# A graph convolution on one core: the shared row is handed on by four products on 32-column tiles instead of one of 128 columns

## What is computed

```python
h = jax.nn.silu(edge_scalars @ fc_w1 * (1.0 / math.sqrt(NES))) * SILU_NORM
w = h @ fc_w2 * (1.0 / math.sqrt(FCN))            # four weights of 64 for each edge
xg0, xg1 = y0[edge_src], y1[edge_src]             # rows gathered for each edge
mids = ...                                        # 8 blocks of 64, products of w, xg, edge_attr
agg = jax.ops.segment_sum(mids, edge_dst, num_segments=n)
```

## Time and profile before

| | |
|---|---|
| median of 3 runs | 4682.87 us (4681.94 to 4685.75) |
| span of the profiled execution | 4674.3 us, from the first to the last instruction |
| TensorE busy (PE) | 4274.9 us, 91% |
| VectorE busy (DVE) | 3652.6 us, 78% |
| GpSimd busy (POOL) | 3308.2 us, 71% |
| ScalarE busy (ACT) | 1445.7 us, 31% |
| DMA | 649.74 MB, mean 139 GB/s |

### The profile page before, as it was taken

How to read it: one execution, slowest core, us unless ns; L and a number is a source line. 1 busy time by engine, 2 the same in 40 slices (tenths; PEclk the granted TensorE clock), 3 DMA queues, 4 the chain that set the end, 5 groups by cost and what they waited for, 6 DMA issues and landing times. The chain is left out here.

```text
span 4674.3 us, 104242 instructions
## 1 busy us (share of the span) xinstructions
PE 4274.9 (91%) x30666; PEld 2586.2 (55%) x30666; DVE 3652.6 (78%) x10846; ACT 1445.7 (31%) x3213; POOL 3308.2 (71%) x3483
## 2 busy tenths in 40 slices
PE   7999999999999999997997899899989999999897
PEld 5333333333333333333896666666666666666675
DVE  8777777777777777776675888888888888888887
ACT  4111111111111111111453344444444444444444
POOL 3777777777777777776333777777777777777774
PEclk9999999999999999998997888888888888888888
DMA  7444444444444444444774444444444444444443
GB/s 268 131 132 132 131 131 132 131 131 131 132 132 129 133 131 130 132 132 141 264 293 171 122 124 125 123 125 124 123 125 124 123 125 122 125 123 123 125 122 86
DMA packets 372900, 649.74 MB, mean 139 GB/s; under 512 B 123028, under 2 KB 242918, under 8 KB 372824
## 3 DMA queue, kind: packets, MB, share of 16 engines
q0 software_dynamic: 168960, 476.88, 36.1%
q1 hardware_dynamic: 203864, 171.98, 12.3%
HBM read 546.90 MB, written 101.68 MB: 139 GB/s over the span
## 5 line engine op out<-in xcount | busy, mean ns | idle before, releaser
L887 POOL DMA_INDIRECT sub_xg<-y_rows,sub_meta x1668 | 1594.8, 956 | 513.0 <-issue 430.4
L2047 POOL DMA_INDIRECT ord_xg<-xpa_rows,ord_meta x1666 | 1595.4, 958 | 510.8 <-issue 466.1
L2115 PE MATMUL ord_a<-ord_xg,ord_sel 128*128 128x264 f32 x3332 | 1131.9, 474 | 131.5 <-DVE ord_xg L2478 131.3
L937 PE MATMUL sub_a<-sub_mids,sub_sel 128*32 128x128 f32 (+1 forms) x13344 | 1004.3, 310 | 102.1 <-DVE sub_mids L1096 100.8
L2115 PEld LDWEIGHTS ord_a<-ord_xg,ord_sel 128*128 128x128 f32 x3332 | 715.9, 236 | 268.7 <-DVE ord_xg L2478 143.5
L1096 DVE TENSOR_TENSOR sub_mids<-sub_w,sub_xg 128x384 f32<-128x384 f32 x1668 | 842.0, 545 | 0.0
L1091 DVE TENSOR_TENSOR sub_mids<-sub_w,sub_xg 128x256 f32<-128x256 f32 x834 | 347.9, 417 | 568.5 <-DMA sub_xg<-y_rows,sub_meta 485.6
L1004 ACT ACTIVATE sub_agg_s<-sub_a 128x256 f32<-128x256 f32 x556 | 213.3, 384 | 1738.1 <-PE sub_a L951 1732.4
L937 PEld LDWEIGHTS sub_a<-sub_mids,sub_sel 128*32 128x32 f32 x13344 | 310.1, 108 | 672.0 <-issue 341.3
L917 PE MATMUL sub_w<-sub_fc,sub_ht 64*128 64x256 f32 x3336 | 587.1, 429 | 0.3 <-DVE sub_mids L1096 0.3
L2478 DVE TENSOR_TENSOR ord_xg<-ord_xg,ord_prob 128x1024 f32<-128x1024 f32 x476 | 510.1, 1072 | 0.0
(11 more groups left out here) (194 smaller groups left out, 4339.8 us busy)
## 6 DMA issues: line engine op xcount, KB each, us to landing
sub_sum_rows<-sub_agg_s SPq DMA_DIRECT2D x139, 256.0 KB
sub_xg<-y_rows,sub_meta POOLq DMA_INDIRECT x1668
ord_xg<-xpa_rows,ord_meta POOLq DMA_INDIRECT x1666
ord_x_rows<-x_rows SPq DMA_DIRECT2D x119, 128.0 KB, 2.3
out_dram<-ord_res SPq DMA_DIRECT2D x119, 128.0 KB
xpa_rows<-mid_proj SPq DMA_DIRECT2D x14, 924.0 KB, 5.3
lin_xt<-in_x_t_dram SPq DMA_DIRECT2D x14, 896.0 KB, 11.5
y_rows<-lin_yb SPq DMA_DIRECT2D x14, 896.0 KB, 10.9
```

Of the source, the lines that this page charges most:

```text
L887: nc.gpsimd.indirect_dma_start(xg[:, b, k], None, y, bass.IndirectOffsetOnAxis(ids[:, b, 0, k:k + 1], 0))\
L937: mm = nc.tensor.matmul(a[ROWS * m:ROWS * (m + 1), 0:w].rearrange("p (q f) -> p q f", f=MUL), sel[:, b, k, m], of, start=(j == 0), stop=False,
L2047: nc.gpsimd.indirect_dma_start(xg[:, b, k], None, xpa, bass.IndirectOffsetOnAxis(ids[:, b, k:k + 1], 0))\
L2115: mm = nc.tensor.matmul(psum_a[b % 2][:, 0:WIDE], sel[:, b, k], xg[:, b, k], start=(k == 0), stop=(k == TILES - 1 and not has(i, b, -1)), ...
```

## The change

The hand-on is cut by the four groups of 32 partitions. Instead of one product with 128x128 weights that streams 256 columns, there are four with 128x32 weights, in the order of `add_up`: three stream the 128 columns that their partitions use, the last, for partitions 0 to 31, all 256. The last one carries the signal `summed`. The waits ahead of the hand-on are the same.

```diff
                         pe.wait_ge(copied, GROUP_SUBS * g + s)
-                        nc.tensor.matmul(psum_a[s % 2][:, 0:4 * MUL], hand_col[:, b, s],
-                                         agg_s[:, b if s > 0 else (b - 1) % SUB_TURN, (s - 1) % GROUP_SUBS],
-                                         start=False, stop=True, skip_group_check=True).then_inc(summed, 1)
+                        before = agg_s[:, b if s > 0 else (b - 1) % SUB_TURN, (s - 1) % GROUP_SUBS]
+                        for m in (1, 2, 3, 0):
+                            part, w = slice(ROWS * m, ROWS * (m + 1)), 4 * MUL if m == 0 else 2 * MUL
+                            mm = nc.tensor.matmul(psum_a[s % 2][part, 0:w], hand_col[:, b, s, part], before[:, 0:w],
+                                                  start=False, stop=True, skip_group_check=True)
+                        mm.then_inc(summed, 1)
```

## The result

The changed kernel is slightly slower: 4693.18 us against 4684.81 us, medians of 14 runs each, a ratio of 1.002 (95% interval 1.0013 to 1.0027). That is 6 to 13 us, about the 0.2% that I took as the limit of what can be told. The span of the profiled execution grew from 4674.3 to 4687.9 us; that is more than the medians moved, because the profiled execution of the kernel before was a quick one.

The account below looks back on a forecast made before the run. GpSimd's gathers bound the convolution and hide TensorE's 118 us; 0.5 us of GpSimd's waits and 0.6 us of tail give 1.1 us, so 4682.87 becomes 4681.8 us, range 4676 to 4689.

Parts of the forecast that it names:

- What bounds the convolution: Convolution: GpSimd issues gathers without a pause, 1.262 us a step, 15.14 us a group; TensorE is close but not the bound.
- TensorE's saving: Convolution's hand-on: four products cost 0.43 us together, saving TensorE 0.85 us a group, 118 us over the stage.
- the rival on products that don't overlap: Hand-on: the four products run one behind the other, 1.08 us each hand-on; 143 us more, 4826 us; 2%.
- the estimate beside the sum: Hand-on, by the skill's speedup table: a quarter of 0.43 us, 178 us more gain for TensorE, hidden behind the gathers anyway.
- All of it becomes waiting: Convolution: TensorE's 118 us saved turn into waits for VectorE at L937, from 99.8 to about 218 us.
- The clock falls: Rival, convolution: TensorE's granted clock drops; at 0.85 a group takes 15.96 us, 114 us more, 4797 us; 3%.
- the point of decision: Convolution, in the clock rival: the clock decides only below a mean of 13.57 / 15.14 = 0.90.
- The tail: Behind the convolution's last gather nothing hides TensorE; the shorter hand-on ends the stage 0.6 us earlier.
- The 8.6 us: Whole kernel: the median of runs stands 8.6 us above the profiled span; carried over unchanged to the forecast.
- The stages behind: Mid stage and attention after the convolution run the same program; claimed not to move by more than a few us.
- The rival on TensorE's loop: Convolution: the longer loop outgrows what is held near the engine, a fetch stalls each turn; 133 us more, 4816 us; 3%.
- The range: Whole kernel's time: 4676 to 4689 us, leaving out the rivals, 12% together.

Follow-up runs that it names:

- e3_lead12: The changed kernel with GpSimd allowed two tiles further ahead of TensorE (LEAD 12 for 10); ratio 0.9981 to the kernel before.
- e1_fill: The changed kernel plus one unread product of 128 streamed columns at each hand-on, restoring TensorE's work; ratio 1.0001 to the kernel before.
- e7_before_again: The kernel before, unchanged, one execution for a second profile; 4673.33 us.
- e5: The kernel before, old hand-on, with LEAD 12 for 10; ratio 0.9988 to the kernel before.
- e9: The kernel before with 68 empty instructions ahead of TensorE's convolution; they weren't in the trace, so a copy of the kernel before; ratio 1.0010.
- e11: The kernel before with LEAD 12 and 68 empty instructions that weren't in the trace; ratio 0.9992 to the kernel before.
- e12: The kernel before with 17 small products (68 instructions) at the start of TensorE's convolution program; ratio 1.0005 to the kernel before.
- e14: The kernel before with 17 small products (68 instructions) ahead of TensorE's convolution and LEAD 12; ratio 0.9989 to the kernel before.
- e8: The changed kernel, unchanged, one execution for a second profile; 4692.66 us.
- e10: The changed kernel with 188 empty instructions ahead of TensorE's convolution; they weren't in the trace, so a copy; ratio 1.0025 to the kernel before.
- e2_old128: The kernel before, its one-product hand-on streaming 128 of the 256 columns, the rest left out; ratio 1.0035 to the kernel before.
- e13: The changed kernel with 47 small products (188 instructions) at the start of TensorE's convolution program; ratio 1.0054 to the kernel before.
- e6: The changed kernel with LEAD 12 for 10, run once more; ratio 0.9980 to the kernel before.

## Why the prediction was wrong

**What bounds the convolution** was right: GpSimd's gathers, 1.262 us a step. e3_lead12 and e1_fill show it from both sides, with TensorE busy for 1925.7 and 2006.2 of 2085 us and the last gather at 2190.3 and 2188.6.

**TensorE's saving** was right in each place: the new hand-on costs 0.43, the places take 1.00 and 1.44 us. The busy time in 100 to 2185 us fell by 73.8 us rather than 118, but the changed kernel is 18.9 us behind at the end of that window. Over the same work, from 100 us to the last gather, it fell from 1989.5 to 1932.7, by 56.9 us; 29 x 3.4 = 99 us of it ran at half speed, which is up to 49 us of work drawn out, together up to 106. So the 118 is somewhat too large. The wait at L937 grew by 73 us and not by 118: it is the 56.9 us of work and the 18.9 by which the stage is longer. In the rival on products that don't overlap, 3 x 0.21 + 0.43 is 1.06 as written; 1.08 goes by half of 0.43, and nothing hangs on it. Nor did the hand-on cost a quarter of 0.43, as the estimate beside the sum would have it: one of its four products still streams 256 columns.

**The step that failed** is "All of it becomes waiting", with the price of nothing for the waiting. It had a rival, "The clock falls", at 3% and with two faults. I spoke against it by the longest wait, 2.4 us at a clock of 1.00. That was misread. This wait is the one at the very end, behind the last gather, and the clock of 1.00 is that of the stage up to 2185 us. Timeline of PE before, and the windows around it, columns as in the earlier trace rows:

```profile
2190.68 0.64 PE L937 MATMUL sub_a<-sub_mids,sub_sel 128*32 128x128 f32 x8 [2.36 <-DVE sub_mids L1096]
```
```profile
2187.00:2192.00 5.00, 2.64 (x28) 1.07 (x30) 1.42 (x4) 0.38 (x1) 1.39 (x2) 1.00 0.85 111
2192.00:2200.00 8.00, 6.71 (x44) 2.55 (x41) 2.64 (x6) 0.77 (x2) 0.00 (x0) 0.57 0.12 16
```

The clock fell at 2192.1 us, 1.4 us behind that wait. It is the fall to 0.77 that my own sum of the tail used. So the trace of before held a case for the rival where I took one against it. In the rest of the stage it has hardly any waits of this length (number of waits, and how many of them have a stretch at 1.2 GHz beginning by their end, 100 to 2185 us):

| TensorE's waits | 1.5 to 1.7 us | 1.7 to 1.9 us | over 1.9 us |
|---|---|---|---|
| before | 13, none | 1, none | none |
| after | 26, 4 | 21, 10 | 23, 15 |

The length doesn't decide alone. In e7_before_again a wait of 2.64 us, up to 2190.40, has no fall behind it before 2199.4. And in the eight profiles with the old amount of work on TensorE (before, e1_fill, e5, e7, e9, e11, e12 and e14) 2 of 79 waits of 1.5 to 1.7 us have a stretch by them and 5 of 17 longer ones, in the three of the changed kernel with LEAD 10 (after, e8, e10) 13 of 67 and 87 of 144. Less work between the waits may count too; each run here changed both together, and none tells them apart.

And I put the point of decision at a mean clock of 0.90, where TensorE's work fills a group on average. It decided at 0.98. GpSimd's room is not the group's mean but what lies between a tile's sums and the gather that waits for them. A single stretch of 3.4 us, which draws out TensorE's work by up to 1.7 us just after it has waited, is more than that room (I had given it over 2 us), and since GpSimd never has a pause, what it loses isn't made good. By the profiles it is 0.65 us a stretch, 19 us in all, not the 114 of the rival as I had it.

In the Trainium skill, "TensorE: Matmul & The Clock Gate", the section on HAM oscillation, tells of a kernel whose clock falls in each wait for data; its waits are longer. The direction agrees with e2_old128, in which less work gave 42 stretches. What this case adds is that the clock fell behind waits of 1.5 to 2.2 us.

**The tail** was sized at 0.6 us, with the last hand-on 10.5 us behind the last gather before. Measured, it starts 2215.33 - 2206.6 = 8.7 us behind it. But the kernel before has 9.3 in e7_before_again, since its clock fell only later there, so this is the clock's place and not the four products.

**The 8.6 us** that I carried over from the span to the median were for the most part no property of the kernel: the runs' own spans lie 1.4 to 2.4 us below their times, and the rest is that one quick execution.

**The stages behind**, which I held to be untouched, weren't: from the last gather to the attention's first it became 7.1 us shorter, 5.4 of it in the stage over the nodes. That the stop there is TensorE waiting for its own program fits the record on q8: nine of the 16 profiles have a stop, of 1.1 to 4.1 us, and in each the next product starts 2.8 to 3.0 us behind a 16 KB piece. And e12 and e14 cut it from 3.9 to 1.1 us by 68 more instructions ahead of it. It isn't settled: e2_old128 has the same number of instructions as the kernel before and a stop of 1.5 us, and e13, which by my count brings the old place back, has none. My count may be off, or the time of the fetch matters too.

**The rival on TensorE's loop** looked at the right resource in the wrong place: nothing is fetched in each turn of the convolution, in the changed kernel either (32 and 49 packets).

**The range**, 4676 to 4689 us, which the measured 4693.18 lies above, left out the rivals as whole sizes. It should have asked what a small part of one would cost: 29 stretches instead of a lower clock throughout.

**The version that beats both** is the change with LEAD 12: 0.9981 and 0.9980, some 9 us under the kernel before. LEAD 12 alone brings 0.9988, with an interval that overlaps theirs. The likely rest is the shorter stage over the nodes and not the hand-on's saving, for which nothing waits; but e14, which has the old hand-on, LEAD 12 and most of the shorter stage, came to 0.9989, so this isn't shown.

## What to carry to other kernels

Before you take work off an engine that isn't the bound, ask what it will do instead. On TensorE the answer here was not nothing: its clock fell behind some of the longer waits, and then it was late at a moment, although it had time on average. Compare the delay of one such moment with the room that the bounding engine has in its waits, not with the mean; if the room is short, widen it first (here two tiles of lead, one number), and only then shorten. Before you quote a wait as proof that the clock holds, look where it stands and at the clock just behind it. And don't count a stage as untouched only because its code is: a longer program ahead of it came with a stop of 3.9 us less.

## What the runs showed of the hardware

- The clock fell to 1.2 GHz for 3.4 us behind single waits of 1.5 to 2.2 us, in an engine that was busy for 92% of the stage (1913.0 of 2085 us). In the eight profiles in which TensorE kept its old amount of work it never did so in four (before, e1, e7, e12), and once to three times in the others (e5 three, e14 two, e9 and e11 one).
- Four products on 32-column tiles behind four others of the same kind start while the 256-column product ahead of them still runs (1006.76 beside 1006.77); the widest one sets the step of 0.43 us.
- TensorE stood still for 3.94 us in the midst of its products with no releaser, next to a 16 KB piece on its instruction queue; the piece was moved 2.9 us before it went on, and 2.8 to 3.0 us in all nine profiles that have such a stop.
- The undisturbed steps between GpSimd's gathers were 1.261 us on average in eight of the 16 profiles and 1.263 to 1.264 in the eight others; the change with LEAD 12 is among both (e6, e3).
